# Loading the rows of adj from ScalarE's queue instead of SyncE's

## The chip, the core and the metric

The kernel runs on one core of one Trainium2 chip. The metric is the device time of one execution in microseconds (us); lower is better.

## The reference

The reference is one graph layer with a residual, all in float32, for 4096 nodes with 256 features:

```python
h = jnp.maximum(_layernorm(x, axis=-1), 0.0)
rowsum = adj.sum(axis=1)
d_inv_sqrt = jnp.where(rowsum > 0, rowsum ** (-0.5), 0.0)
normalized_adj = d_inv_sqrt[:, None] * adj * d_inv_sqrt[None, :]
out = normalized_adj @ h @ W + b
return x + relu(out)
```

adj is 4096 x 4096 (64 MiB). The host hands it over twice: `in_adj` as it is, and `in_adj_t`, the same numbers cut into transposed blocks for the product.

## The kernel before

**The data.** adj is read in two forms, and each of them is 64 transfers of 1 MiB.

- The *rows*: transfer m is half of the rows of block m // 2 (128 rows x 2048 columns). It goes to one of LN = 3 buffers `nat`. ScalarE sums it along the row (`sum_nat`, L333 to L336, the row at L335), and GpSimd makes the scale s of block j from the sums 2j and 2j + 1 (`scale_of`, L456 to L468, some 2 us).
- The *blocks*: transfer g is slot g of the transposed matrix, in one of LA = 4 buffers `at`. ScalarE rounds it to `hi` (`round_slot`, L338; L348 in the narrow steps, which also scales by s, L343 in the wide ones), VectorE subtracts to get the rest, `lo` (`subtract`, L536; L544 and L548), and that subtraction frees the buffer. `hi` and `lo` have RING = 3 buffers each.

**The product.** TensorE multiplies slot after slot, 24 matmuls of 128x512 for each (L696, L697, L698: G's upper part by hi, by lo, G's lower part by hi). There are 64 slots in 11 steps. Steps 0 to 5 are *narrow*: 4 slots each, two blocks of rows wide. Steps 6 to 10 are *wide*: 8 slots each, four blocks wide. The first twelve blocks of G are unscaled (`round_raw`, `rest_of_raw`), with s applied to the slots; from block 12 on, G itself is scaled by VectorE (`make_G`, L530 and L532), so step 6, which begins with slot 24, needs G's blocks 12 to 15 and with them the sums up to 31. Before slot 0, TensorE turns and projects five chunks of h (`turn` L650, `project` L666).

**ScalarE's order** is written out by hand: two copies of turned chunks, then sum 0, round_raw 0, sum 1, take_turned 2, sum 2, round_raw 1, take_turned 3, sum 3, round_raw 2, take_turned 4, slot 0, take_product 3, slot 1, take_product 4 (L365). Slot 0 of the product on TensorE waits for take_product 4. Then it loops over the slots g: in a narrow step the sums NATS[g] and then the rounding of slot g + 2, in a wide step the rounding first. Rounding slot g + 2 waits until TensorE is done with slot g - 1. NATS holds 2, 2, 0, 0 sums in the four slots of a narrow step, but 2, 3, 3, 0 in step 5 (sums 24 to 31, at g = 20, 21, 22), and at most 2 for a slot in the wide steps.

**SyncE's order.** All transfers are issued by SyncE, one after the other, on one queue: x chunks 0 and 1, W, x chunks 2 and 3, rows 0 and 1, x chunk 4, rows 2 and 3, slots 0 and 1, b; then over g, in a narrow step the rows NATS[g] and then slot g + 2, in a wide step the slot first. A load of rows m waits for sum m - 3 (`nat_summed`); while it waits, everything behind it in SyncE's order waits too. Slots 2 and 3 wait for turned chunks, since their buffers hold chunks of h at first; later slots wait for the subtraction of the slot four before.

**VectorE's order** at the border of the narrow and the wide steps: two gathers of TensorE's panels (L563) and the subtraction of slot 24, G's block 12, two gathers, the subtraction of slot 25, G's blocks 13, 14 and 15, the subtraction of slot 26.

In the text below, "rows m", "sum m" and "slot g" are these transfers and instructions.

Of the kernel before, what the change touches and what calls it, by code (L numbers as in the profile page):

```python
# [13 lines left out]
DMA = 16  # L14
# [8 lines left out]
WIDTHS = [2, 2, 2, 2, 2, 2, 4, 4, 4, 4, 4]  # L23
NP = 8
NB = 32
# [4 lines left out]
NARROW = [w == 2 for w in WIDTHS]  # L30
# [16 lines left out]
def slot_table():  # L47
    table = []
    for k, width in enumerate(WIDTHS):
        n = SLOT // width  # L50
        order = panel_order(k)
        for q in range(NP // n):
            table.append((k, q, order[q * n:(q + 1) * n]))
    return table


SLOTS = slot_table()
# [14 lines left out]
NATS = nat_table()  # L72
# [27 lines left out]
def at_least(eng, sem, value):  # L100
    if value > 0:
        eng.wait_ge(sem, value)


def build(nc, x, x_t, adj, adj_t, w, b, out):
# [3 lines left out]
    LN = 3  # L109
# [5 lines left out]
    adj_rows = adj.rearrange("(j p) (c k) -> j c p k", p=P, k=HALF)  # L115

    with ExitStack() as ctx:
# [34 lines left out]
        nat = [sb(f"nat{e}", [P, HALF]) for e in range(LN)]  # L152
# [48 lines left out]
        x_landed = [sem(f"x_landed{e}") for e in range(AHEAD)]  # L201
        w_landed = sem("w_landed")
        b_landed = sem("b_landed")
        nat_landed = [sem(f"nat_landed{e}") for e in range(LN)]
# [13 lines left out]
        nat_summed = sem("nat_summed")  # L218
# [53 lines left out]
        @block.sync  # L272
        def _(sp):
            def load_x(c):
                if c >= AHEAD:
                    sp.wait_ge(G_ready, G_count(BW * (c - 1) - 1))
                sp.dma_start(h(c), x[c]).then_inc(x_landed[c % AHEAD], DMA)

            def load_nat(m):
                at_least(sp, nat_summed, m - LN + 1)  # L280
                sp.dma_start(nat[m % LN][:, :], adj_rows[m // 2, m % 2]).then_inc(nat_landed[m % LN], DMA)

            def load_slot(g):
                if g in (2, 3):
                    sp.wait_ge(h_turned, 2 * (g - 1))
                at_least(sp, lo_ready, pieces(g - LA))
                sp.dma_start(at[g % LA][:, :, :], adj_t[g]).then_inc(at_landed[g % LA], DMA)

            load_x(0)
            load_x(1)  # L290
            sp.dma_start(w_sb[:, :, :], w.rearrange("(f p) n -> p f n", p=P)).then_inc(w_landed, DMA)
            load_x(2)
            load_x(3)
            for m in range(2 * WIDTHS[0]):
                load_nat(m)
                if m == 1:
                    load_x(4)
            load_slot(0)
            load_slot(1)
            sp.dma_start(b_sb[:, :], b).then_inc(b_landed, DMA)  # L300
            order = panel_order(LAST)
            for g, (k, q, _) in enumerate(SLOTS):
                if k == LAST and q == 1:
                    sp.wait_ge(nat_summed, 2 * NB)
                    sp.wait_ge(G_ready, G_count(NB - 1))
                    for pos in range(LX):
                        sp.dma_start(x_out(pos), x_t[order[pos]]).then_inc(x_out_landed[pos], DMA)
                if q == 2 and chunk_of(k) is not None:
                    load_x(chunk_of(k))
                if not NARROW[k]:  # L310
                    if g + 2 < len(SLOTS):
                        load_slot(g + 2)
                for m in NATS[g]:
                    load_nat(m)
                if NARROW[k]:
                    load_slot(g + 2)
            for pos in range(NP - 1):
                sp.wait_ge(out_ready, pos + 1)
                sp.dma_start(out[order[pos]], x_out(pos)).then_inc(stored[pos % LX], DMA)
                if pos + LX < NP:  # L320
                    sp.wait_ge(stored[pos % LX], DMA * (pos // LX + 1))
                    sp.dma_start(x_out(pos), x_t[order[pos + LX]]).then_inc(x_out_landed[pos % LX], DMA)
            for f in range(FD):
                sp.wait_ge(out_ready, NP + f)
                sp.dma_start(out[order[NP - 1], :, f, :],
                             x_out(NP - 1)[:, f, :]).then_inc(stored[(NP - 1) % LX], DMA)
            for e in range(LX):
                pieces_stored = len(range(e, NP, LX)) + (FD - 1 if e == (NP - 1) % LX else 0)
                sp.wait_ge(stored[e], DMA * pieces_stored)

        @block.scalar
        def _(act):
            def sum_nat(m):  # L333
                act.wait_ge(nat_landed[m % LN], DMA * (m // LN + 1))
                nc.scalar.activation(nat[m % LN][:, :], nat[m % LN][:, :], ACT.Copy,  # L335
                                     accum_out=part[:, m // 2, m % 2:m % 2 + 1]).then_inc(nat_summed, 1)  # L336

            def round_slot(g):  # L338
                k = SLOTS[g][0]
                act.wait_ge(at_landed[g % LA], DMA * (g // LA + 1))  # L340
                at_least(act, panel_done, slot_done(g - RING))
                if not NARROW[k]:
                    nc.scalar.copy(hi[g % RING][:, :, :], at[g % LA][:, :, :]).then_inc(hi_ready, 1)  # L343
                    return
                for c in range(2):
                    j = FIRST[k] + c
                    act.wait_ge(s_ready, j + 1)
                    nc.scalar.activation(hi[g % RING][:, 2 * c:2 * c + 2, :], at[g % LA][:, 2 * c:2 * c + 2, :],  # L348
                                         ACT.Copy, scale=s[:, j:j + 1]).then_inc(hi_ready, 1)

            def take_turned(c):
                act.wait_ge(h_turned, c + 1)
                if 2 <= c < AHEAD:
                    act.wait_ge(hW_done, c - 1)
                nc.scalar.copy(hT(c), pair_of(("turn", c))[:, :, :]).then_inc(hT_ready, 1)

            def round_raw(c):

                act.wait_ge(hW_done, c + 1)
                nc.scalar.copy(G[:, BW * c:BW * (c + 1), 0, :],  # L360
                               held[c % 2][:, :, :].rearrange("p a (t f) -> p (a t) f", f=D)).then_inc(raw_hi_made, 1)

            def take_product(c):
                act.wait_ge(hW_done, c + 1)
                nc.scalar.copy(hW(c), chunk_product(c)[:, :, :].rearrange("p a (t f) -> p (a t) f", f=D)  # L365
                               ).then_inc(hW_ready, 1)

            def take_d_rows(r):
                act.wait_ge(d_turned, r + 1)
                act.wait_ge(nat_summed, 2 * NB)  # L370
                nc.scalar.copy(d_rows(r), pair_of(("d_row", r))[:, :, :]).then_inc(d_row_ready, 1)

            def rectify(pos, f):
                act.wait_ge(scaled, FD * pos + f + 1)
                nc.scalar.activation(total(pos)[:, f, :], total(pos)[:, f, :], ACT.Relu,  # L375
                                     bias=b_sb[:, f:f + 1]).then_inc(rectified, 1)

            take_turned(0)
            take_turned(1)
            sum_nat(0)  # L380
            round_raw(0)
            sum_nat(1)
            take_turned(2)
            sum_nat(2)
            round_raw(1)
            take_turned(3)
            sum_nat(3)
            round_raw(2)
            take_turned(4)
            round_slot(0)  # L390
            take_product(3)
            round_slot(1)
            take_product(4)
            for g, (k, q, _) in enumerate(SLOTS):
                c = chunk_of(k)
                if NARROW[k]:
                    for m in NATS[g]:
                        sum_nat(m)
                if g + 2 < len(SLOTS):
                    round_slot(g + 2)  # L400
                if c is not None and q == 5:
                    take_turned(c)
                if not NARROW[k]:
                    for m in NATS[g]:
                        sum_nat(m)
                if c is not None and q == 6:
                    take_product(c)
                if k == LAST:
                    if q == 0:
                        act.wait_ge(b_landed, DMA)  # L410
                    else:
                        for f in range(FD):
                            rectify(q - 1, f)
                    if q % 2 == 0:
                        take_d_rows(q // 2)
            for f in range(FD):
                rectify(NP - 1, f)
# [349 lines left out]
```

## Time and profile before

| | before |
|---|---|
| median of 3 runs | 416.89 us (416.85 to 418.31) |
| the profiled execution | 419.11 us, its span 417.3 us |
| TensorE busy | 393.9 us (94%) |
| ScalarE, VectorE, GpSimd busy | 281.3, 286.3, 137.1 us |
| DMA | 147.39 MB, mean 353 GB/s |

The span runs from the first to the last instruction; the time of the execution holds 1.8 us more around it. TensorE is busy nearly throughout, so what a change is worth has to be looked for in its few idle stretches and in what could make new ones.

### The profile page before, as it was taken

The page shows a single profiled execution, that of the slowest core. Times are in us where ns is not written, and L with a number is a line of the kernel's source. Part 1 is how long each engine was busy: PE and PEld are TensorE (multiplying, and loading weights), DVE is VectorE, ACT ScalarE, POOL GpSimd, SP SyncE. Part 2 cuts the span into 40 slices and gives each one's busy share as a digit, 9 for nine tenths or more (in the row PEclk, how much of TensorE's full clock was granted, in tenths as well). Part 3 has the DMA queues.
Part 4 walks back from the last instruction along what each step waited for, and adds up shares of the span by engine and source line. Part 5 has one row for each costly group of instructions (what it writes and reads, how often), then busy time and mean ns, then how long its engine had stood idle before and what let it go on. Part 6 is the DMA issues. An engine that isn't in the chain of part 4 may idle for free.

```text
span 417.3 us, 4994 instructions
## 1 busy us (share of the span) xinstructions
PE 393.9 (94%) x1760; PEld 326.9 (78%) x1760; DVE 286.3 (69%) x286; ACT 281.3 (67%) x253; POOL 137.1 (33%) x303
## 2 busy tenths in 40 slices
PE   2998999999999998599999999999999999997995
PEld 2887888888888876388888888888888888886884
DVE  6644878879696945928745596547846477749984
ACT  1899786959696878477655867487665877345542
POOL 3233535343133233013610354011810211635650
PEclk9999999999999999899999999999999999998999
DMA  8997999998989899999986999599994996296663
GB/s 322 422 418 311 426 419 422 381 426 342 426 342 428 337 408 424 395 418 423 421 371 223 404 426 423 205 354 413 425 421 146 390 425 277 97 393 234 205 227 155
DMA packets 22473, 147.39 MB, mean 353 GB/s; under 512 B 2608, under 2 KB 2864, under 8 KB 6064
## 3 DMA queue, kind: packets, MB, share of 16 engines
q1 hardware_dynamic: 22448, 147.07, 87.3%
q8 instruction: 14, 0.23, 0.2%
q14 instruction: 11, 0.09, 0.1%
HBM read 142.87 MB, written 4.19 MB: 352 GB/s over the span
## 4 chain that ended last, share of the span: by engine, by line
PE 84%; DMA 7%; DVE 3%; ACT 2%; issue 2%; SPq 0%; DVEq 0%; ACTq 0%
PE moved L696 18%; PE moved L697 18%; PE moved L698 18%; PE held L696 7%; PE held L697 7%; PE held L698 7%; DMA at<-in_adj_t 5%; PE held L666 4%; PE moved L666 2%; PE moved L650 2%; DMA nat<-in_adj 2%; ACT hi L343 1%; DVE acc L563 1%; PE moved L712 1%; DMA at<-in_x 1%
## 5 line engine op out<-in xcount | busy, mean ns | idle before, releaser
L696 PE MATMUL moved<-hi,G 128*128 128x512 f32 x384 | 151.2, 394 | 0.7 <-DVE acc L563 0.7
L697 PE MATMUL moved<-lo,G 128*128 128x512 f32 x384 | 149.9, 390 | 0.0
L698 PE MATMUL moved<-hi,G 128*128 128x512 f32 x384 | 149.7, 390 | 0.0
L335 ACT ACTIVATE nat<-nat 128x2048 f32<-128x2048 f32 x64 | 122.2, 1911 | 6.8 <-DMA nat<-in_adj 6.8
L548 DVE TENSOR_TENSOR lo<-at,hi 128x2048 fp32r<-128x2048 f32 x40 | 91.8, 2295 | 48.6 <-ACT hi L343 48.6
L343 ACT CAST hi<-at 128x2048 fp32r<-128x2048 f32 x40 | 76.4, 1909 | 66.7 <-PE moved L698 47.9
L563 DVE TENSOR_TENSOR acc<-moved,acc 128x1024 f32<-128x1024 f32 x60 | 73.3, 1222 | 51.3 <-PE moved L698 51.3
L696 PEld LDWEIGHTS moved<-hi,G 128*128 128x128 f32 x384 | 72.4, 189 | 15.9 <-DVE acc L563 1.1
L698 PEld LDWEIGHTS moved<-hi,G 128*128 128x128 f32 x384 | 72.3, 188 | 15.2
L697 PEld LDWEIGHTS moved<-lo,G 128*128 128x128 f32 x384 | 72.4, 189 | 14.8
L459 POOL TENSOR_TENSOR row_sum<-part 128x1 f32<-128x1 f32 x32 | 9.8, 306 | 203.9 <-ACT nat L335 203.9
L348 ACT ACTIVATE hi<-at,s 128x1024 fp32r<-128x1024 f32 x48 | 52.7, 1148 | 21.4 <-issue 15.1
L544 DVE SCALAR_TENSOR_TENSOR lo<-at,s,hi 128x1024 fp32r<-128x1024 f32 x48 | 60.3, 1279 | 9.3 <-ACT hi L348 9.3
L696 PE MATMUL held<-hi,G 128*128 128x512 f32 x128 | 50.9, 397 | 7.6 <-DVE G L532 6.5
L697 PE MATMUL held<-lo,G 128*128 128x512 f32 x128 | 50.5, 395 | 0.0
L698 PE MATMUL held<-hi,G 128*128 128x512 f32 x128 | 50.3, 393 | 0.0
L696 PEld LDWEIGHTS held<-hi,G 128*128 128x128 f32 x128 | 24.4, 190 | 13.9 <-DVE G L532 4.0
L476 POOL TENSOR_SCALAR turned<-ident,d 128x128 f32<-128x128 f32 x32 | 27.2, 853 | 19.0 <-PE moved L712 16.6
L698 PEld LDWEIGHTS held<-hi,G 128*128 128x128 f32 x128 | 24.5, 191 | 5.2
L697 PEld LDWEIGHTS held<-lo,G 128*128 128x128 f32 x128 | 24.4, 191 | 5.0
L463 POOL TENSOR_TENSOR row_pow<-row_safe,minus_half 128x1 f32<-128x1 f32 x32 | 22.7, 709 | 2.7
L375 ACT ACTIVATE acc<-acc,b_sb 128x512 f32<-128x512 f32 x16 | 10.9, 717 | 13.5 <-DVE acc L578 13.5
(54 smaller groups left out, 261.7 us busy)
## 6 DMA issues: line engine op xcount, KB each, us to landing
nat<-in_adj SPq DMA_DIRECT2D x64, 1024.0 KB, 10.3
at<-in_adj_t SPq DMA_DIRECT2D x64, 1024.0 KB, 10.5
nat<-in_x_t SPq DMA_DIRECT2D x6, 512.0 KB, 3.6
out<-nat SPq DMA_DIRECT2D x5, 512.0 KB, 3.7
at<-in_x SPq DMA_DIRECT2D x4, 512.0 KB, 5.0
turned<-in_x SPq DMA_DIRECT2D x3, 512.0 KB, 3.9
turned<-in_x_t SPq DMA_DIRECT2D x2, 512.0 KB, 5.2
out<-turned SPq DMA_DIRECT2D x2, 512.0 KB, 3.8
```

The costliest lines, as they stand in the source:

```text
L335: nc.scalar.activation(nat[m % LN][:, :], nat[m % LN][:, :], ACT.Copy, accum_out=part[:, m // 2, m % 2:m % 2 + 1]).then_inc(nat_summed, 1)
L343: nc.scalar.copy(hi[g % RING][:, :, :], at[g % LA][:, :, :]).then_inc(hi_ready, 1)
L348: nc.scalar.activation(hi[g % RING][:, 2 * c:2 * c + 2, :], at[g % LA][:, 2 * c:2 * c + 2, :], ACT.Copy, scale=s[:, j:j + 1]).then_inc(hi_ ...
L463: then(nc.gpsimd.tensor_tensor(out=row_pow[:, one], in0=row_safe[:, one], in1=minus_half[:, 0:1], op=ALU.pow))
L476: wide = nc.gpsimd.tensor_scalar(d_wide(pos, t), ident[:, :], 0.0, d[:, j:j + 1], ALU.mult, ALU.add)
L544: nc.vector.scalar_tensor_tensor(out=lo[g % RING][:, tiles, :], in0=at[g % LA][:, tiles, :], scalar=s[:, j:j + 1], in1=hi[g % RING][:, til ...
L548: nc.vector.tensor_tensor(out=lo[g % RING][:, :, :], in0=at[g % LA][:, :, :], in1=hi[g % RING][:, :, :].bitcast(F32), op=ALU.subtract).the ...
L563: nc.vector.tensor_tensor(out=own, in0=pair[:, :, :], in1=own, op=ALU.add).then_inc(taken, 1)
L666: mm = nc.tensor.matmul(chunk_product(c)[:, a, t * D:(t + 1) * D], hT(c)[:, f, tile * P:(tile + 1) * P], w_sb[:, f, :], start=(f == 0), st ...
L696: nc.tensor.matmul(into[:, f, :], big, hi[g % RING][:, t, :], start=begins, stop=False)
L697: nc.tensor.matmul(into[:, f, :], big, lo[g % RING][:, t, :], start=False, stop=False)
L698: mm = nc.tensor.matmul(into[:, f, :], small, hi[g % RING][:, t, :], start=False, stop=ends)
```

## The change

The 64 loads of rows move from SyncE's instruction stream to ScalarE's. Rows 0, 1 and 2 are issued by ScalarE as soon as x chunk 1 has landed, ahead of all its work. Rows m + 2 are issued by ScalarE at the head of sum m, before it waits for rows m; the semaphore wait of the load (sum m - 1 is done) stays. So the load is the next instruction behind sum m - 1 only where sums follow each other; where a rounding or a copy stands between them, the load comes behind that. SyncE's stream keeps x, W, b, the slots and the output. x chunk 4 and slots 0 and 1 now follow x chunk 3 directly. In every step the slot loads wait only for their own buffer.

```diff
@@ block.sync
-            def load_nat(m):
-                at_least(sp, nat_summed, m - LN + 1)
-                sp.dma_start(nat[m % LN][:, :], adj_rows[m // 2, m % 2]).then_inc(nat_landed[m % LN], DMA)
...
             load_x(3)
-            for m in range(2 * WIDTHS[0]):
-                load_nat(m)
-                if m == 1:
-                    load_x(4)
+            load_x(4)
             load_slot(0)
             load_slot(1)
...
-                if not NARROW[k]:
-                    if g + 2 < len(SLOTS):
-                        load_slot(g + 2)
-                for m in NATS[g]:
-                    load_nat(m)
-                if NARROW[k]:
+                if g + 2 < len(SLOTS):
                     load_slot(g + 2)
@@ block.scalar
+            def load_nat(m):
+                at_least(act, nat_summed, m - LN + 1)
+                act.dma_start(nat[m % LN][:, :], adj_rows[m // 2, m % 2]).then_inc(nat_landed[m % LN], DMA)
+
             def sum_nat(m):
+
+                if LN <= m + LN - 1 < 2 * NB:
+                    load_nat(m + LN - 1)
                 act.wait_ge(nat_landed[m % LN], DMA * (m // LN + 1))
...
+            act.wait_ge(x_landed[1], DMA)
+            for m in range(LN):
+                load_nat(m)
             take_turned(0)
```

## Rows read from the trace of the kernel before

**Rows 1.** The page: DMA queues, and issues with their time to landing.

```profile
q1 hardware_dynamic: 22448, 147.07, 87.3%
...
nat<-in_adj SPq DMA_DIRECT2D x64, 1024.0 KB, 10.3
```

**Rows 2.** Waits of TensorE, 30 to 417 us: total, times, longest.

```profile
PE held L696 <- DVE G L532: 6.5, 2, 3.5
PE moved L712 <- DVE acc L563: 2.4, 1, 2.4
```

**Rows 3.** Stretches of 8 us: busy by engine, granted clock, DMA share, GB/s.

```profile
24.00:32.00 8.00, 8.00 (x42) 7.10 (x42) 4.36 (x4) 8.00 (x9) 1.59 (x6) 1.00 1.02 417
...
168.00:176.00 8.00, 4.11 (x12) 3.07 (x13) 7.89 (x11) 3.91 (x3) 0.00 (x0) 0.85 0.99 409
176.00:184.00 8.00, 8.00 (x34) 6.50 (x34) 3.51 (x2) 4.42 (x4) 0.44 (x2) 0.93 1.01 400
```

**Rows 4.** Waits of SyncE's queue, whole span: total, times, longest.

```profile
SPq L281 <- ACT nat L335: 211.0, 52, 13.5
...
SPq L305 <- DVE G L532: 16.9, 1, 16.9
```

**Rows 5.** SyncE's loads of rows, L281: duration in ns, time to landing.

```profile
L281 SPq DMA_DIRECT2D nat<-in_adj x64: 327/328/612, 3.1 to 338.0; - x64
...
DMA to landing us min/median/max: 5.1/10.3/15.6
```

**Rows 6.** Timeline 0 to 40 us, the start.

```profile
4.15 2.73 DVE L509 BATCH_NORM_STATS2 stats<-at 128x6 f32<-128x256 f32 x8 [4.15 <-DMA at<-in_x]
...
15.07 0.91 SPq L287 DMA_DIRECT2D at<-in_adj_t  x2
15.22 1.40 DVE L509 BATCH_NORM_STATS2 stats<-acc 128x6 f32<-128x256 f32 x4 [1.50 <-DMA acc<-in_x]
...
16.93 1.91 ACT L335 ACTIVATE nat<-nat 128x2048 f32<-128x2048 f32 x1
...
23.43 1.94 ACT L335 ACTIVATE nat<-nat 128x2048 f32<-128x2048 f32 x1
...
32.46 1.01 ACT L365 COPY turned<-held 128x1024 f32<-128x1024 f32 x1
...
33.53 0.50 PE L696 MATMUL held<-hi,G 128*128 128x512 f32 x1 [1.10 <-ACT turned L365]
```

**Rows 7.** Timeline of ScalarE, 115 to 164 us: sums 24 to 31 and roundings.

```profile
115.52 2.20 ACT L348 ACTIVATE hi<-at,s 128x1024 fp32r<-128x1024 f32 x2 [3.24 <-issue]
...
137.28 2.20 ACT L348 ACTIVATE hi<-at,s 128x1024 fp32r<-128x1024 f32 x2 [3.24 <-issue]
139.38 1.90 ACT L335 ACTIVATE nat<-nat 128x2048 f32<-128x2048 f32 x1
...
150.76 1.92 ACT L335 ACTIVATE nat<-nat 128x2048 f32<-128x2048 f32 x1 [1.63 <-DMA nat<-in_adj]
...
158.21 1.92 ACT L335 ACTIVATE nat<-nat 128x2048 f32<-128x2048 f32 x1 [0.48 <-DMA nat<-in_adj]
...
160.71 1.92 ACT L335 ACTIVATE nat<-nat 128x2048 f32<-128x2048 f32 x1 [0.49 <-DMA nat<-in_adj]
...
163.18 1.91 ACT L343 CAST hi<-at 128x2048 fp32r<-128x2048 f32 x1 [0.47 <-DMA at<-in_adj_t]
```

**Rows 8.** Timeline of SyncE, 120 to 155 us: slots 24 to 26 last.

```profile
153.17 1.38 SPq L287 DMA_DIRECT2D at<-in_adj_t  x3
```

**Rows 9.** Timeline of VectorE, 140 to 182 us.

```profile
143.81 3.67 DVE L544 SCALAR_TENSOR_TENSOR lo<-at,s,hi 128x1024 fp32r<-128x1024 f32 x3
...
165.12 2.29 DVE L548 TENSOR_TENSOR lo<-at,hi 128x2048 fp32r<-128x2048 f32 x1 [3.94 <-ACT hi L343]
```

**Rows 10.** Timeline of TensorE, 150 to 182 us: first matmuls behind the waits.

```profile
168.34 0.47 PE L696 MATMUL held<-hi,G 128*128 128x512 f32 x1 [2.98 <-DVE G L532]
...
173.50 0.68 PE L696 MATMUL held<-hi,G 128*128 128x512 f32 x1 [3.54 <-DVE G L532]
```

## The prediction

> **What bounds the kernel now.** I read the page first. All bulk transfers run on one queue, busy 87% of the span, and a load of rows lands 10.3 us after its issue in the median: the queue is deep [rows 1]. TensorE is busy 94% of the time, so I listed what it waits for once slot 0 has begun. Only two entries matter: 6.5 us for G's blocks at the border of the narrow and the wide steps, and 2.4 us near the end [rows 2]. By the 8 us stretches the clock fell after the first from 2.4 to 1.2 GHz for part of the time, 0.85 and 0.93 of full: (0.15 + 0.07) x 8 = 1.8 us more [rows 3]. Outside of these, slots follow each other on TensorE every 5.44 us (the roundings at 115.52 and 137.28, which by the code wait for it, stand four slots apart, [rows 7]), and any gain must come from these places. The same view shows that from 24 to 32 us TensorE, ScalarE and the DMA engines are all full [rows 3]. There a little more work on ScalarE, or rows that land late, has no cover.
>
> **What is removed.** SyncE spent 211 us in waits for sums [rows 4]. These go, and slots no longer stand behind them. That alone gives TensorE nothing: among its waits there is none for a late slot [rows 2]. The wait near the end hangs on SyncE's x_t loads, which wait 16.9 us for G's last block [rows 4]; that block is paced by TensorE, and neither the wait nor its place in SyncE's order is touched. I count 0 there.
>
> **The price of an issue on ScalarE.** No row has one. The nearest is SyncE's issue of the same load, 0.33 us [rows 5]. Below, it may be 0, if ScalarE's queue works it off beside the instruction that runs; above, 0.33 plus the drain of the sum before it, some 0.2, where two sums stand back to back. I take 0.33, and 0.55 between two sums. Over 64 loads that is 21 to 35 us on an engine with 417.3 - 281.3 = 136 us idle. It is hidden everywhere but at the two places below, and in them it is small beside the landings.
>
> **Part one, the start.** I measure transfers in jobs of 1 MiB. Successive landings at the border are 2.5 us apart (158.21, 160.71, both released by a landing [rows 7]), so a job takes 2.5 us and an x chunk 1.25. x chunk 0 lands at 4.13 and x chunk 4, behind four x chunks, W and two rows (4.75 jobs with its own), at 15.2 [rows 6]; so a transfer lands at about 3.1 + 2.5 x (jobs up to and with it). Before, rows 0 to 3 are all issued ahead of slots 0 and 1, which go out at 15.07 [rows 6]; rows 3 are number 6.75 and land near 20, ahead of sum 3 at 23.43.
>
> After, SyncE has nothing to wait for up to slot 1: x chunk 4, slots 0 and 1 are issued by some 4.5 us, at 0.46 us each (two slots took 0.91, [rows 6]). x chunk 1 lands at 5.6 and only then does ScalarE issue rows 0, 1, 2. Slot 2 joins when two chunks are turned (near 12), slot 3 when four are (near 21). Rows 3 go out at the head of sum 1 (16.93 before, [rows 6]). So slots 0, 1 and 2, three jobs that nobody needs before 27 us, compete with the rows that ScalarE needs from 12.7 us on.
>
> The trace has one queue, so no row shows how two are served. The ends: ScalarE's queue first, when every landing is in time and only three issues remain, +1.0 us; or all in order of issue. In order of issue rows 0 land at 3.1 + 2.5 x 5.75 = 17.5, rows 2 at 22.5; sum 1, held by round_raw 0, starts at 20.9, so rows 3 land at 27.5 behind slot 2, and sum 3, behind copies that are late too, starts at 28.5, +5.1. Between them: halves for each from the moment that both have work. The rows' progress begins near 8.0 (issue at 5.6 and the 2.4 to 2.6 us that the shortest landing, 5.1 us, holds beyond its 2.5 [rows 5]); at 5 us each they land at 13.0, 18.0, 23.0 and 28.0. Sums 0 and 1 slip by 0.4 and 1.1 us, sum 2 by 3.4, sum 3 by 28.0 - 23.4 = 4.6. Halves and issue order nearly agree, and I take 4.6.
>
> Does it reach TensorE? From sum 3 to take_product 4 (23.43 to 32.46, [rows 6]) ScalarE has no idle time, and slot 0 starts at 33.53 behind that copy [rows 6]. TensorE's own work is no cover: project 4 needs round_raw 2 and take_turned 4, both behind sum 3. So slot 0 starts at about 38.1. **Term one: +4.6 us** (bounds +0.4 to +5.5; the lower one with issues at half their price).
>
> The Trainium skill ("DMA: Bandwidth & Descriptors", section "Queues, rings and completion order") says that each DMA engine takes turns between the queues with work, packet by packet. By this rule the sum is the one by halves. "Issuing engines are not separate DMA queues" on the same page speaks against the change: transfers of all issuers interleave on the same engines. No row here shows either.
>
> **Part two, narrow steps 0 to 4.** Rows m + 2 now go out at the head of sum m. Where roundings stand between sum m - 1 and sum m (two slots of each narrow step), that is later than before: of three buffers, one stays empty for up to two slots. Each step moves 8 jobs, 20 us in 4 x 5.44 = 21.8 us. My walk has the fourth sum of a step 1 to 2 us later; the rounding behind it is needed some 5 us afterwards. Price 0.
>
> **Part three, the border.** Step 5 sums eight rows in three slots. Before, rows 26 were already there at 139.4, and nothing of slots 24 to 26 was issued before 153.2 [rows 8]; rows 28 to 31, with slot 23 between, landed back to back, and sum 31 started at 160.71 [rows 7]. The rounding of slot 24 followed at 163.18 and released the subtraction at 165.12, with which VectorE's closed chain begins that ends both TensorE waits [rows 7, 9, 10]. So TensorE moves one for one with that rounding.
>
> After, in the times of before (a shift of slot 0 moves all of it alike, since ScalarE and the buffers are paced by TensorE): the rounding at 137.28 stays, sum 24 and the issue of rows 26 come at 139.4, rows 27 at 141.8. Slot 24 is issued when slot 20 is subtracted, 139.6 (5.44 before slot 21's end at 145.1, the first of three in [rows 9]), slot 25 at 145.1, slot 26 near 147.6. A fresh transfer starts to progress 2.6 us after its issue. By halves: rows 26 land at 146.9; rows 27 at 151.2 (2.5 us alone is 5 us shared with slots 24 and 25); rows 28, issued at 146.2, at 156.2, beside slots 25 and 26; rows 29 at 159.5, rows 30 at 162.0. Sum 28 is at 156.2 instead of 150.76, the rounding of slot 23 ends at 160.3, and only then are rows 31 issued: landing 160.3 + 5.1 = 165.4. Sum 31 takes 2.0 us, and slot 24 is rounded at 167.4, **term two: +4.2 us**. In order of issue the same walk gives 166.5, +3.3. The lower bound: no sharing and free issues. Rows 28 issued at 145.3 land at 150.4, slot 23 is rounded by 154.4, rows 31 land at 159.5, slot 24 is rounded at 161.5: -1.7. The upper one, with the clock low for as long again as now (+1.8), is +6.
>
> **The sum.** 4.6 + 4.2 = +8.8 us. Against the profiled execution (419.11 us, span 417.3) that is 427.9, span 426.1. That execution lies 2.2 us above the median of the runs, 416.89; from the median it is 425.7 us, +2.1%.
>
> **The rivals.**
>
> *The start alone.* The border's sharing is milder: slots 24 to 26 land in the gaps. Then 4.6 and about 1 for issues: 422.5. For it: only three slots stand against six rows. Against: they are issued right then.
>
> *The border alone.* ScalarE's queue gets its rows early, since few packets wait in it; the start costs 1.0. Then 1.0 + 3.3 to 4.2: some 421.5. For it: the start's slots have 10 us of slack. Against: nothing gives the rows precedence.
>
> *Hidden.* Bandwidth goes to who needs it, both terms fall to their issue prices, 0 to +1.5 us: 417.6. For it: 136 us idle on ScalarE and slots four deep. The change would then do what it says, and gain nothing, as no slot was late.
>
> *Faster.* At the border DMA is the limit: rows 28 to 31 come in at its full rate, with slot 23 between them. Slot 23 could now load ahead, and the chain above falls to its lower bound: 1.7 us earlier, and with a shorter wait up to 1.8 us of low clock go too. That is -1.7 to -3.5: 413.4 to 415.2. It decides if sum 31 starts 1 us or more ahead of its place relative to TensorE's slots, the clock stays up and the start loses nothing. Against: rows 26 are issued 11 us later than before (behind sum 23 then, at sum 24 now).
>
> **How the numbers follow.** Half a per cent, 2.1 us, is what a measurement of this kernel can tell from no change. Chances: both terms 0.48 (its own range 422 to 430), the start alone 0.17, the border alone 0.12, hidden 0.16, faster 0.07. So slower 0.77, same 0.16, faster 0.07. The range leaves out the faster case, the lower half of the hidden one and the far end of the first: 417.5 to 430.
>
> **What would show it.** Right: sum 3 starts between 27 and 29 us and slot 0 near 38; slots 0 and 1 issued before 5 us; at the border sum 31 and the rounding of slot 24 later against the end of slot 23, TensorE's wait there for G 6 us or more; slots 24 and 25 issued before rows 30; the DMA share below 1 between 30 and 40 us, where the rows wait for ScalarE. Wrong: rows 0 to 2 landing 2.5 us apart though slots are queued; an issue on ScalarE far above 0.33 us, with which the error is upward; waits of TensorE at the start that pull its clock to 1.2 GHz, likewise; or a sum 31 that keeps its place.

## The result, and the profile after

The changed kernel takes 430.52 us (median of 4 runs, 428.31 to 432.19) against 417.38 us before (4 runs, 416.85 to 418.31): 1.030 times as long, with a 95% interval of 1.0249 to 1.0352. The profiled execution took 431.15 us, its span is 429.3 us, 12.0 more than before. One run, of the kernel "rows of the wide steps only" below, took 507.2 us at a mean granted clock of 0.756 and is left out of all figures.

The page after has two bulk queues where there was one [rows 1]:

```profile
q1 hardware_dynamic: 13232, 79.96, 47.5%
q10 hardware_dynamic: 9216, 67.11, 38.4%
...
at<-in_adj_t SPq DMA_DIRECT2D x64, 1024.0 KB, 9.7
nat<-in_adj ACTq DMA_DIRECT2D x64, 1024.0 KB, 9.8
```

The median time from issue to landing is no longer than before: 9.7 and 9.8 us, against 10.3 for rows [rows 1]. The median hides where it became longer. TensorE's waits after 30 us answer to [rows 2] (total, times, longest):

```profile
PE moved L694 <- DVE acc L561: 5.4, 2, 5.0
PE held L694 <- DVE G L530: 4.5, 2, 3.5
PE moved L694 <- DVE acc L558: 2.5, 1, 2.5
...
PE moved L710 <- DVE acc L561: 1.8, 1, 1.8
```

Two of them are new: the first, at the border, and the third, in slot 2. ScalarE, which waited 6.8 us in nine places for rows before, now has

```profile
ACT nat L330 <- DMA nat<-in_adj: 35.1, 27, 3.3
...
ACT nat L330 <- ACT nat L330: 4.1, 10, 0.4
```

To see where TensorE fell behind, I took every 24th matmul of the product, which is the start of a slot, from the timelines of both kernels:

```
slot                before    after    behind by   added since
0                    33.53    36.87      3.34        3.34
2                    44.55    47.93      3.38        0.04
3                    49.99    57.75      7.76        4.38
10                   88.07    95.83      7.76        0
11                   93.51   101.95      8.44        0.68
22                  153.35   162.22      8.87        0.43
23                  159.76   174.30     14.54        5.67
24                  168.34   180.90     12.56       -1.98
25                  179.33   191.86     12.53       -0.03
46                  303.25   316.61     13.36        0.83
58                  372.89   386.28     13.39        0.03
59                  383.46   394.70     11.24       -2.15
63                  407.03   418.41     11.38        0.14
```

**The start: +3.3 us.** ScalarE's timeline after. Its queue issues three loads at 5.31, and the sums wait for them:

```profile
5.31 1.54 ACTq L323 DMA_DIRECT2D nat<-in_adj  x3
...
14.53 1.92 ACT L330 ACTIVATE nat<-nat 128x2048 f32<-128x2048 f32 x1 [1.93 <-DMA nat<-in_adj]
...
19.50 1.92 ACT L330 ACTIVATE nat<-nat 128x2048 f32<-128x2048 f32 x1 [2.06 <-DMA nat<-in_adj]
...
22.99 1.91 ACT L330 ACTIVATE nat<-nat 128x2048 f32<-128x2048 f32 x1 [0.59 <-DMA nat<-in_adj]
...
27.03 1.91 ACT L330 ACTIVATE nat<-nat 128x2048 f32<-128x2048 f32 x1 [0.22 <-DMA nat<-in_adj]
```

Rows 0 and 1 land 5.0 us apart while SyncE's queue also has work; with the one queue of before, successive loads stood 2.5 us apart [rows 7]. Slots 0 and 1 were issued at 3.60 us, 11.5 us earlier than before [rows 6]. Sum 3 slips by 27.03 - 23.43 = 3.6 us, slot 0 of the product by 3.3.

**Slot 2: +4.4 us.** ScalarE's timeline again: rows 6 and 7 are issued at 35.01 and 38.75, at the heads of sums 4 and 5, and both take 9.0 us to land.

```profile
35.01 0.34 ACTq L323 DMA_DIRECT2D nat<-in_adj  x1
...
38.75 0.33 ACTq L323 DMA_DIRECT2D nat<-in_adj  x1
...
44.00 1.92 ACT L330 ACTIVATE nat<-nat 128x2048 f32<-128x2048 f32 x1 [0.77 <-DMA nat<-in_adj]
...
47.76 1.92 ACT L330 ACTIVATE nat<-nat 128x2048 f32<-128x2048 f32 x1 [1.76 <-DMA nat<-in_adj]
...
49.67 4.25 ACT L343 ACTIVATE hi<-at,s 128x1024 fp32r<-128x1024 f32 x4
```

The same places of the kernel before, SyncE's issue of rows 6 and ScalarE's rounding of slot 3 (two views, so two fences):

```profile
25.48 10.25 SPq L281 DMA_DIRECT2D nat<-in_adj  x2
```

```profile
43.07 2.20 ACT L348 ACTIVATE hi<-at,s 128x1024 fp32r<-128x1024 f32 x2
```

Slot 3 is rounded 6.6 us later, from 49.67 on: 3.3 of them are the start, 3.3 are new. TensorE would reach slot 3 only at 49.99 + 3.38 = 53.4, but VectorE works in order: the gather that frees a `moved` buffer stands behind slot 3's first subtraction. VectorE and then TensorE after:

```profile
50.84 1.28 DVE L542 SCALAR_TENSOR_TENSOR lo<-at,s,hi 128x1024 fp32r<-128x1024 f32 x1 [4.21 <-PE moved L696]
52.04 1.22 DVE L558 COPY acc<-moved 128x1024 f32<-128x1024 f32 x1
```

```profile
53.32 0.62 PE L694 MATMUL moved<-hi,G 128*128 128x512 f32 x1 [2.51 <-DVE acc L558]
```

(The releaser named for the 4.21 us is a matmul, but VectorE's own order has it wait for hi of slot 3, at 50.8.) The stretches show what else it cost: the granted clock fell to 1.2 GHz for part of the time behind the wait, (0.15 + 0.06) x 8 = 1.7 us.

```profile
48.00:56.00 8.00, 5.49 (x20) 4.09 (x19) 5.16 (x5) 5.92 (x6) 5.28 (x13) 0.85 0.75 294
56.00:64.00 8.00, 8.00 (x35) 6.59 (x34) 6.24 (x6) 5.59 (x5) 0.23 (x1) 0.94 0.92 340
...
168.00:176.00 8.00, 5.91 (x20) 4.82 (x21) 5.59 (x5) 6.81 (x8) 1.79 (x7) 0.79 0.98 380
```

**The border: +3.7 us** (5.67 in slot 22, of which 2.0 come back). ScalarE's timeline: sums 28 to 31, the roundings of slots 23 and 24.

```profile
164.54 1.91 ACT L330 ACTIVATE nat<-nat 128x2048 f32<-128x2048 f32 x1 [2.96 <-DMA nat<-in_adj]
...
166.45 1.13 ACT L343 ACTIVATE hi<-at,s 128x1024 fp32r<-128x1024 f32 x1
...
173.83 1.92 ACT L330 ACTIVATE nat<-nat 128x2048 f32<-128x2048 f32 x1 [0.44 <-DMA nat<-in_adj]
...
175.74 3.71 ACT L338 CAST hi<-at 128x2048 fp32r<-128x2048 f32 x2
```

Set back by the 8.87 us that slot 22 is late, sum 28 is at 155.7 (150.76 before), sum 31 at 165.0 (160.71) and the rounding of slot 24 at 166.9 (163.18, [rows 7]), 3.7 us later. TensorE, in the same view, first loses 5.0 us in slot 22 to VectorE's order as in slot 2, and then less in front of slot 24; its wait for G's block 13 is as long as before [rows 10].

```profile
170.09 0.80 PE L694 MATMUL moved<-hi,G 128*128 128x512 f32 x1 [4.99 <-DVE acc L561]
...
180.90 0.47 PE L694 MATMUL held<-hi,G 128*128 128x512 f32 x1 [0.99 <-DVE G L530]
...
186.05 0.50 PE L694 MATMUL held<-hi,G 128*128 128x512 f32 x1 [3.53 <-DVE G L530]
```

**The end: -2.2 us**, which is no gain of the change. The wait that hangs on the x_t loads stays (1.8 us, 2.4 before), but in this profile of before the clock fell behind it, and in the one after it did not. First before, then after:

```profile
376.00:384.00 8.00, 5.83 (x23) 4.99 (x24) 7.08 (x7) 3.07 (x5) 3.68 (x3) 0.79 0.73 258
```

```profile
384.00:392.00 8.00, 6.16 (x32) 4.94 (x31) 5.51 (x5) 5.17 (x5) 0.00 (x0) 1.00 1.00 382
```

### The profile page after: what moved, and what is told of

The parts are those of the page before. It is cut to its first block, busy times and chain, and to the rows that moved or that the text cites. A ratio compares the mean times of both kernels' runs of the same rounds, so it can differ in the third digit from the quotient of the medians.

```text
span 429.3 us, 4994 instructions
## 1 busy us (share of the span) xinstructions
PE 397.0 (92%) x1760; PEld 327.1 (76%) x1760; DVE 285.6 (67%) x286; ACT 282.3 (66%) x253; POOL 148.3 (35%) x303
## 4 chain that ended last, share of the span: by engine, by line
PE 60%; DMA 21%; issue 7%; ACT 6%; DVE 5%; SPq 1%; DVEq 0%; ACTq 0%
PE moved L694 14%; PE moved L695 14%; PE moved L696 14%; DMA nat<-in_adj 10%; PE held L694 5%; DMA out<-nat 5%; PE held L696 5%; PE held L695 5%; PE moved L664 2%; DMA at<-in_adj_t 2%; DVE acc L561 2%; ACT hi L343 2%; ACT hi L338 2%; DMA out<-turned 2%; ACT nat L330 1%
## 5 line engine op out<-in xcount | busy, mean ns | idle before, releaser
L457 POOL TENSOR_TENSOR row_sum<-part 128x1 f32<-128x1 f32 x32 | 13.7, 429 | 218.4 <-ACT nat L330 218.4
L474 POOL TENSOR_SCALAR turned<-ident,d 128x128 f32<-128x128 f32 x32 | 28.6, 895 | 16.2 <-PE moved L710 13.9
L664 PE MATMUL held<-w_sb,turned 128*128 128x256 f32 x80 | 19.0, 391 | 2.2 <-ACT turned L350 1.8
```

The source lines that it names most:

```text
L457: then(nc.gpsimd.tensor_tensor(out=row_sum[:, one], in0=part[:, j, 0:1], in1=part[:, j, 1:2], op=ALU.add))
L474: wide = nc.gpsimd.tensor_scalar(d_wide(pos, t), ident[:, :], 0.0, d[:, j:j + 1], ALU.mult, ALU.add)
L664: mm = nc.tensor.matmul(chunk_product(c)[:, a, t * D:(t + 1) * D], hT(c)[:, f, tile * P:(tile + 1) * P], w_sb[:, f, :], start=(f == 0), st ...
```

## The experiments

The table splits each profile by TensorE's slot starts, as above: how far behind the profile of before it is at slot 0, what slots 0 to 21, the border (22 to 24) and the rest add, and the difference of the spans. The time is the median of the runs; the ratio is to runs of the kernel before that were measured beside them. Where the time and the one profile disagree, the time counts. In the profile of before the clock was low near the end, so a kernel whose own profile kept the clock there has some -2 us under "rest". The changed kernel and the one with the edit "G early" run the same code up to the border, and lost 5.5 and 7.7 us in slots 0 to 21: so much can one profile of a two-queue kernel differ from another.

| kernel | start | slots 0-21 | border | rest | span | time, ratio (95%) |
|---|---|---|---|---|---|---|
| after | 3.3 | 5.5 | 3.7 | -1.2 | +12.0 | 430.52, 1.030 |
| start gated | 0.1 | 6.4 | 2.7 | -1.3 | +8.4 | 429.99, 1.028 (1.022-1.034) |
| all gated | 1.1 | 4.0 | 4.4 | -0.3 | +9.2 | 428.13, 1.024 (1.020-1.028) |
| issue behind the sum | 4.1 | 1.8 | 4.2 | -1.8 | +8.6 | 428.37, 1.024 (1.019-1.029) |
| both | 0.5 | 6.4 | 4.0 | -0.4 | +10.5 | 429.12, 1.025 (1.019-1.031) |
| before + small issues | 0.2 | 1.8 | 0.7 | -2.1 | +0.7 | 420.22, 1.006 (1.003-1.009) |
| before, slot between | 0.4 | 0.0 | -0.6 | -2.0 | -1.4 | 417.59, 1.000 (0.996-1.004) |
| before, G early | -0.6 | 0.0 | -5.3 | 1.3 | -4.5 | 414.41, 0.991 (0.988-0.994) |
| before, between and G early | 0.0 | 0.0 | -5.5 | -1.9 | -6.9 | 412.57, 0.988 (0.982-0.994) |
| after, G early | 3.7 | 7.7 | -0.3 | -0.8 | +10.2 | 428.27, 1.024 (1.016-1.033) |
| before, slots cut | -0.3 | 0.0 | -3.1 | -3.2 | -6.5 | 412.66, 0.988 (0.983-0.993) |
| after, slots cut | 4.5 | 0.6 | -1.2 | -3.9 | 0.0 | 419.08, 1.003 (1.000-1.007) |
| before, rows of the wide steps only | | | | | | 419.09, 1.002 (0.998-1.005) |

**Slots 0 and 1 held back at the start.**

```diff
             load_x(4)
+            sp.wait_ge(nat_summed, 1)
             load_slot(0)
```

> The changed kernel, but SyncE holds slots 0 and 1 back until sum 0 is done, as in the kernel before; all later slots stay free. Theory (slots ahead of the rows): slot 0 of the product starts within 1 us of 33.5 instead of 36.9, and the wait of TensorE at slot 2 (4.4 us with its low clock) shrinks, since rows 3 to 7 move up: 422 to 425 us. Rival (price of the issues on ScalarE): the start stays near 36.9 and the time near 430. The border (5.7 us of wait at slot 22) stays in both.

The start did what the theory said: slot 0 begins 0.1 us behind before instead of 3.3. Rows 0 and 1 land 2.5 us apart again (13.1 and 15.6). So the start's loss was slots ahead of rows. The forecast of the time was a miss: 430.0. The transfers of slots 0 and 1 now stand later, in front of what comes next, and slot 2 lost 6.1 us instead of 4.4. ScalarE's sum 7 in this kernel:

```profile
46.28 1.92 ACT L331 ACTIVATE nat<-nat 128x2048 f32<-128x2048 f32 x1 [3.54 <-DMA nat<-in_adj]
```

Rows 7 went out at 35.5 us and took 10.7 us to land, beside slots 4 and 5, which had gone out at 31.2 and 34.2.

**All slots held back as before.** SyncE waits at each slot for the sums that it waited for when it loaded the rows itself.

```diff
+                if NARROW[k]:
+                    for m in NATS[g]:
+                        at_least(sp, nat_summed, m - LN + 1)
                 if g + 2 < len(SLOTS):
                     load_slot(g + 2)
+                if not NARROW[k]:
+                    for m in NATS[g]:
+                        at_least(sp, nat_summed, m - LN + 1)
```

> The changed kernel, but every slot waits on SyncE for the same sums as in the kernel before, so that no slot runs ahead of the rows that stood in front of it; rows stay on ScalarE, issued at the head of sum m - 2. Theory A (slots running ahead take the bandwidth): the start and the border both come back to within 1 or 2 us of before, 418 to 420 us. Theory B (rows are issued too late, behind roundings): the start comes back, but the border keeps 3 us or more, 421 to 424 us.

**Rows issued directly behind the sum that frees the buffer.**

```diff
             def sum_nat(m):
-                if LN <= m + LN - 1 < 2 * NB:
-                    load_nat(m + LN - 1)
                 act.wait_ge(nat_landed[m % LN], DMA * (m // LN + 1))
...
+                if m + LN < 2 * NB:
+                    load_nat(m + LN)
```

> The changed kernel, but rows m + 3 are issued directly behind sum m (with the wait for its end) instead of at the head of sum m + 1; slots stay free. Theory A (slots running ahead): the start stays near +3.3 us, the border loses little, 426 to 430 us. Theory B (issued too late): the waits at slots 2 and 22 go, only the start stays, 419 to 422 us.

**Both edits.**

> Both edits: slots gated as before and rows issued directly behind the sum. The order of the transfers is then nearly that of the kernel before, from two queues. Both theories: 417 to 419 us; what is left over the kernel before is the price of 64 issues on ScalarE where it has no idle time. If it stays above 421, sharing between two queues or the issue itself costs by itself.

None of the three gives back much. Their medians lie 1.4 to 2.4 us below the changed kernel's, and the intervals of the four ratios overlap, so it is not shown that any of it is a gain. With the slots held back neither theory's time was met. With rows issued behind the sum theory A's time was met (426 to 430 us), but not its small loss at the border: the border costs 4.0 to 4.4 us in all three. Both edits together missed their 417 to 419 us by 10. Their expectation names what is then left: the sharing, or the issue itself.

The kernel with both edits shows the sharing by itself, since its rows and slots go out in nearly the old order. Slot 2 costs it 0.5 us. It loses 1.6 in slot 0, at the low clock behind a first wait of 1.9 us, and 4.3 in slot 10. There rows 15 and slot 11 wait for the same sum. In one queue they go out one behind the other and land in that order. In two queues they go out within 0.03 us of each other (80.69 and 80.72) and land together. The issues of these two transfers and their time to landing, with both edits and then before:

```profile
nat<-in_adj ACTq DMA_DIRECT2D x1, 1024.0 KB, 9.1
at<-in_adj_t SPq DMA_DIRECT2D x1, 1024.0 KB, 8.8
```

```profile
nat<-in_adj SPq DMA_DIRECT2D x1, 1024.0 KB, 6.6
at<-in_adj_t SPq DMA_DIRECT2D x1, 1024.0 KB, 8.7
```

The slot lands as fast as before, the rows 2.5 us later, and sum 15, which ScalarE has to do before it rounds slot 11, waits 2.1 us for them instead of 0.8. So the landing of rows that went out in the same moment as a slot is late by the slot's own 2.5 us. Rows 15 had also gone out 2 us late against TensorE's slots, since an earlier rounding waited 2.8 us for slot 9: slots come late too. This kernel's waits of ScalarE:

```profile
ACT hi L349 <- DMA at<-in_adj_t: 13.1, 6, 3.0
...
ACT nat L334 <- DMA nat<-in_adj: 11.9, 10, 2.7
```

At the border rows 31 land at 171.2, and of the slots that follow one ends a wait at 176.37 and the next at 181.35, 5.0 us apart, where before they stood 2.5 apart:

```profile
171.22 1.92 ACT L334 ACTIVATE nat<-nat 128x2048 f32<-128x2048 f32 x1 [2.69 <-DMA nat<-in_adj]
...
176.37 1.90 ACT L344 CAST hi<-at 128x2048 fp32r<-128x2048 f32 x1 [0.78 <-DMA at<-in_adj_t]
181.35 1.90 ACT L344 CAST hi<-at 128x2048 fp32r<-128x2048 f32 x1 [3.08 <-DMA at<-in_adj_t]
```

How much of the loss is the issue on ScalarE, and how much the sharing of the DMA engines by two queues? The next runs ask that.

**The issue alone.**

```diff
             def sum_nat(m):
+                if m:
+                    at_least(act, nat_summed, m)
+                    act.dma_start(spare[:, m, :], b).then_inc(spare_landed, DMA)
                 act.wait_ge(nat_landed[m % LN], DMA * (m // LN + 1))
```

> The kernel before, rows still loaded by SyncE in its order; only ScalarE issues a 1 KB transfer of b into a spare tile at the head of every sum but the first (with the same wait for the sum before), 63 in all, which nothing reads. It pays the issues on ScalarE without a second bulk queue. Theory A (two bulk queues share, and each transfer lands later): 1 us or less over before at the start, at most 1.5 us at the border, 418 to 420 us. Theory B (the issue itself, and the wait for the sum's end, stall ScalarE): most of the loss is here, 424 us or more.

420.22 us, +0.6%: just above theory A's 418 to 420, and far from theory B's. On ScalarE the timeline shows both prices of an issue. The one at 35.56 waits for the sum that runs, and the next sum starts 2.47 us behind that one, 0.6 more than the 1.9 of before; the one at 38.01 has its wait fulfilled, is worked off while a rounding runs, and costs nothing.

```profile
33.50 1.95 ACT L340 ACTIVATE nat<-nat 128x2048 f32<-128x2048 f32 x1
...
35.56 0.36 ACTq L338 DMA_DIRECT2D spare<-in_b  x1
35.97 1.92 ACT L340 ACTIVATE nat<-nat 128x2048 f32<-128x2048 f32 x1 [0.44 <-ACT nat L340]
...
37.88 1.14 ACT L353 ACTIVATE hi<-at,s 128x1024 fp32r<-128x1024 f32 x1
38.01 0.36 ACTq L338 DMA_DIRECT2D spare<-in_b  x1
38.92 1.14 ACT L353 ACTIVATE hi<-at,s 128x1024 fp32r<-128x1024 f32 x1
...
45.48 2.19 ACT L353 ACTIVATE hi<-at,s 128x1024 fp32r<-128x1024 f32 x2 [0.89 <-DMA at<-in_adj_t]
```

But the run does not price the issue alone. Its bulk loads land later too: rows 11.9 us after their issue in the median, 10.3 before; rows 7, issued at 35.56 (35.40 before), took 7.0 us instead of 5.2. The 1.8 us in slot 2 are mostly that: in the last line the rounding of slot 3 waits for its transfer. So 2.4 us of the 13 (1.1 to 3.9 by its interval) is an upper figure for the issues. Whether the small transfers delayed the bulk loads was not separated from a slow start of the profiled execution: W, loaded before any of them, took 7.2 us to land instead of 4.8.

**A slot ahead of rows, one queue.** In the second slot of each narrow step (the condition is put in words here):

```diff
-                for m in NATS[g]:
+                for m in NATS[g][:1] if <second slot of a narrow step> else NATS[g]:
                     load_nat(m)
                 if NARROW[k]:
                     load_slot(g + 2)
+                if <second slot of a narrow step>:
+                    for m in NATS[g][1:]:
+                        load_nat(m)
```

> The kernel before, one queue; in the second slot of each narrow step SyncE loads the slot behind the first row instead of behind the last. That gives one slot per narrow step the freedom that the change gives to all, without a second queue. Theory A: no loss, 415 to 418 us, since nothing shares. Theory B (a slot ahead of the rows costs whatever the queue): slot 23 stands ahead of rows 27, the border is 1 to 2.5 us later, 418 to 420 us.

No loss: 417.59 us, ratio 1.000, theory A. One slot per step that passes rows does no harm where one queue works them off one by one.

**Rows of the wide steps only.** Rows 36 to 63 are loaded by ScalarE, the others stay with SyncE.

```diff
             def sum_nat(m):
+                if 36 <= m + LN - 1 < 2 * NB:
+                    e = m + LN - 1
+                    act.wait_ge(nat_summed, m)
+                    act.dma_start(nat[e % LN][:, :], adj_rows[e // 2, e % 2]).then_inc(nat_landed[e % LN], DMA)
```

> The kernel before, but rows 36 to 63, those of the wide steps, are loaded by ScalarE at the head of sum m - 2; rows 0 to 35 stay with SyncE. There ScalarE idles over 1 us in each slot and DMA has gaps. Theory A (the loss is all in the narrow steps): 416.5 to 418.5 us. Theory B (two queues cost everywhere, as lower bandwidth or as issues): 28 of 64 loads, 2 us or more of the loss, 419.5 us or more.

The median of 419.09 us lies between the two theories' figures; the ratio is 1.0015 (0.9982 to 1.0049). So there is no loss that this measurement can tell, with 28 of the 64 issues and transfers moved, and at most some 2 us; 28/64 of 13.1 would be 5.7. The loss is not spread evenly over the loads. That nothing waits for them in the wide steps was not looked at in a profile of this kernel.

**G's blocks made together.** In place of one block behind slot 24's subtraction and three behind slot 25's:

```diff
-                last = BASE[k + 1] - 1
-                table.setdefault(min(g + 2, last), []).append(m // 2)
+                last = BASE[k + 1] - 1
+                at = min(g + 2, last) if k + 1 > 6 else BASE[6] - 2
+                table.setdefault(at, []).append(m // 2)
```

> The kernel before, but VectorE makes G's blocks 12 to 15 all directly behind the subtraction of slot 24, ahead of the two gathers and the subtraction of slot 25. If the second wait at the border (3.5 us, then half clock) is VectorE's order and not a late transfer, it goes, and with it most of 1.8 us of low clock: 412 to 414 us. If transfers hold it, no change.

> The kernel before with both edits that cost nothing or gained: the slot behind the first row in the second slot of each narrow step, and G's blocks 12 to 15 made together. If the first wait at the border is transfers and the slot in between helps them, 412 to 414 us, below the kernel with G early alone; if not, the same as that one, 414 to 415 us.

> The changed kernel with G's blocks 12 to 15 made together. The gain should be that of the kernel before, 3 to 5 us: 426 to 428 us. What stays over the kernel before with the same edit is then the change's own loss, 12 to 13 us.

On the kernel before it gains 0.9% (414.41 us, just above the forecast), and with the slot in between 1.2%: 412.57 us, the fastest kernel here. Most of the second wait at the border was VectorE's order. On TensorE, 1.1 us stay of the 3.5:

```profile
166.67 0.47 PE L697 MATMUL held<-hi,G 128*128 128x512 f32 x1 [2.86 <-DVE G L533]
173.49 0.47 PE L697 MATMUL held<-hi,G 128*128 128x512 f32 x1 [1.09 <-DVE lo L549]
```

The slot in between adds a gain by the medians (412.57 against 414.41), and in its profile the first wait at the border is 1.5 us instead of 2.9, but the intervals of the two ratios overlap. On the changed kernel the same edit gives 428.27 us in two runs, 2.3 less than without where I had expected 3 to 5; the change stays 13.9 us behind its counterpart, where I had expected 12 to 13.

**The slots cut.** From slot 4 on only a quarter of each slot is transferred, in both kernels, and the product is then of old numbers. Instructions, waits and issues are the same.

```diff
-                sp.dma_start(at[g % LA][:, :, :], adj_t[g]).then_inc(at_landed[g % LA], DMA)
+                part_of = slice(0, 1 if g >= LA else SLOT)
+                sp.dma_start(at[g % LA][:, part_of, :], adj_t[g][:, part_of, :]).then_inc(at_landed[g % LA], DMA)
```

> The changed kernel, but from slot 4 on only the first quarter of each slot is transferred (the rest of the buffer keeps old numbers, so the product is of other data); all instructions, waits and issues stay. Theory A (sharing of the DMA engines in the narrow steps): with the load on them gone, the waits at slots 2 and 22 go nearly wholly; what stays is the start, +3.3 us (slots 0 to 3 are whole), and the issues. Theory B (issues, or the late place of the issue in ScalarE's order): rows still go out late, 8 us or more over the kernel before with the same cut.

> The control: the kernel before with the same cut of the slots' transfers from slot 4 on. The first wait at the border (3.0 us), which late transfers make, should go: 412 to 415 us. The change under the cut is the difference of the two: 3 to 6 us by theory A, 8 or more by theory B.

The change costs 419.08 - 412.66 = 6.4 us under the cut, against 13.1 without, a little above theory A's 3 to 6. By the table 4.7 of the 6.5 in the spans are the start (4.45 + 0.25), whose slots 0 to 3 are whole; slots 0 to 21 add 0.6 instead of 5.5, though rows 6 and 7 still go out late (36.1 and 39.9). The border costs 1.9 us more than in the control, against 3.7. The control itself was 412.66, as forecast, but not for the forecast reason: its first wait at the border is still 2.4 us of 3.0. In the changed kernel with the cut the wait in slot 2 is all but gone:

```profile
PE held L695 <- DVE G L531: 5.9, 2, 3.5
...
PE moved L695 <- DVE acc L559: 0.3, 1, 0.3
```

## Why the prediction was right, and where it was short

The direction and the two places were right; the size was too small: +8.8 us forecast, +13.1 measured, 430.5 against 425.7, just above the range's upper end of 430.0. (The range was set from a median of 416.89. As a ratio its end is 1.031, and 1.030 was measured.) That it came so near is in part luck: a term put at nothing cost 5.5 us, the first term was 1.3 too large, and the profile shows 1.2 less behind the border for a reason that is not the change's.

**Term one, the start: 4.6 forecast, 3.3 measured** (3.3 to 4.5 in the four profiles with an open start). The split by halves was right: rows 0 and 1 landed 5.0 us apart. Rows 0 to 3 were summed at 14.5, 19.5, 23.0 and 27.0 where I had them at 13.0, 18.0, 23.0 and 28.0. Holding slots 0 and 1 back took the loss away. The Trainium skill ("DMA: Bandwidth & Descriptors", section "Queues, rings and completion order") says that each DMA engine takes turns between the queues that have work. The trace agrees, with landings 5.0 us apart against 2.5; it does not show the turns themselves.

**Term two, the border: 4.2 forecast, 3.7 measured.** Sum 31 was forecast at 165.4 and was at 165.0 in the times of before, slot 24's rounding at 167.4 and was at 166.9. Slots 24, 25 and 26 went out at 148.85, 153.99 and 156.38, within 0.4 us of the walk (139.6, 145.1, 147.6, plus 8.87). So the step held, but that it is right to 0.4 us is partly luck. Rows 31 did not go out behind the rounding of slot 23 but beside its first half, at 166.58, 2.6 us before the walk's 160.3 + 8.87; and they took 7.2 us instead of 5.1. The two errors cancel. The early slots are not the whole cause either: with all slots held back the border costs 4.4 us. With the slots' bytes cut it costs 1.9.

One reading was wrong, without effect on the sum: rows 26 were not there at 139.4 in the kernel before. They were issued at 128.44 and landed 15.3 us later, at 143.7, still ahead of sum 26 at 145.25. And two signs did not say what they should. TensorE's wait for G was to be 6 us or more and was 4.5, since TensorE lost most of the term in slot 22 already, through the gather behind slot 23's subtraction. The DMA share between 32 and 40 us was 0.89, below 1 as forecast, but it had been 0.73 in the kernel before.

**Part two, the narrow steps: 0 forecast, 5.5 measured.** This is the step that failed, in three ways. I wrote that the fourth sum of a step would be 1 to 2 us late. That was walked for a step in the middle, where the profile after loses next to nothing (0.7 in slot 10, 0.4 in slot 18). In step 0 rows 6 and 7 go out at 35.0 and 38.8 instead of 25.5 and 35.4, land beside slots 4 and 5, and the fourth sum and the rounding of slot 3 are 6.6 us late, 3.3 of it their own. I wrote that the rounding had some 5 us until it was needed. That was the wrong deadline: not TensorE's need of slot 3, but VectorE's gather, queued behind slot 3's subtraction. And on top of the 2.5 us of wait comes the low clock, 1.7 us. In slot 2 both the late issue and the traffic count: with rows issued behind the sum it costs 1.8 us, with the slots' traffic cut 0.6. But the late issue is not needed for a loss in these steps: the kernel with both edits loses 6.4 us in them.

**The issues on ScalarE.** 0.33 us each, and 0.5 to 0.6 us between two sums, as forecast; the other half of the choice, that a queue may work it off beside the instruction that runs, was also true. In the profile after the waits behind a sum add up to 4.1 us in ten places. "Small beside the landings" was right: 2.4 us at most, out of 13.

**The removed waits of SyncE** gave nothing, as forecast.

**The rivals.** Hidden, faster, and the two single-term cases are all out. What lay outside of all of them was a third place. With it the sum at the last slot is 3.34 + 5.53 + 3.66 - 1.15 = 11.38, and 0.63 more behind the last slot: the 12.0 of the spans.

**What stays open.** How the 13 us split between sharing and the late place of the issues cannot be said to the microsecond: the two feed each other, and one profile of a two-queue kernel differs from the next by 2 us in slots 0 to 21. The kernel with both edits, whose order is nearly that of before, is 11.5 us slower than the runs beside it, of which at most 2.4 are issues by the run with small transfers. The remaining 9 I put down to sharing: pairs of a rows and a slot transfer that land together, and landings 5.0 us apart, show it at work, but what each pair cost TensorE was not added up. Two bulk queues without issues on ScalarE were not tried.

## What to carry to other kernels

A second queue adds no bandwidth where the first one already fills the DMA engines; it gives up the order. In one queue the transfer needed first lands first, at full rate; in two, both land when the later one would have (9.1 and 8.8 us here, instead of 6.6 and 8.7). Issuing in the right order does not bring the order back. Before moving loads, write down for each one when it is needed and what it will then run beside, and look for the deadline not only at the consumer but at every instruction that stands behind the waiting one in its engine's order: here VectorE's gather, which holds TensorE's buffer. In the wide steps the same move cost nothing that could be measured (at most 0.5%), and gained nothing either.

## What the runs showed of the hardware

- Two queues with 1 MiB loads each: landings 5.0 us apart in each of them, against 2.5 us in one queue. The rate of the engines together is the same: in the 8 us stretches with a DMA share of 1.00 or more the median is 423 GB/s with one queue and 424 with two.
- ScalarE issues a load in 0.33 us, as SyncE does (0.33, [rows 5]). With its semaphore wait already fulfilled it costs ScalarE nothing; behind the sum that it waits for it costs 0.5 to 0.6 us (2.43 and 2.47 us from one sum to the next, 1.91 before).
- A wait of 2.5 us on TensorE was followed by eight matmuls 0.43 us apart (1.2 GHz) before the usual 0.23 (2.4 GHz), and the stretch behind the 3.5 us wait at 186 shows a mean of 0.79; the wait of 1.8 us near the end was followed by full speed, the 2.4 us one of before at the same place was not. So a short new wait can cost nearly twice its length: 4.4 us in slot 2 for 2.5 of wait.
